# Four of eight row blocks turned by VectorE and through DRAM instead of by TensorE, and the first layer in a new order

## What is computed

```python
h = relu(layernorm(x))
q, k, v = h @ Wq + bq, h @ Wk + bk, h @ Wv + bv
adj = zeros(N, N); adj[src, dst] = 1
a = (q @ k.T) / sqrt(512) * adj + (1 - adj) * -1e6
x = x + softmax(a) @ v
h = relu(layernorm(x))
agg = segment_sum(h[src], dst) / max(degree, 1)
x = x + h + alpha * (agg @ W.T + b)
```

## Time and profile before

| | us |
|---|---|
| median of 3 runs | 228.92 (228.65 to 229.41) |
| the profiled execution | 228.71 |
| its span | 226.9 |
| first projection G0 of the first layer starts | 26.77 |
| first scores start | 85.44 |

### The profile page before, as it was taken

How to read it: one execution, slowest core, us unless ns; L and a number is a source line. 1 busy time by engine, 2 the same in 40 slices (tenths; PEclk the granted TensorE clock), 3 DMA queues, 4 the chain that set the end, 5 groups by cost and what they waited for, 6 DMA issues and landing times.

```text
span 226.9 us, 3216 instructions
## 1 busy us (share of the span) xinstructions
PE 222.7 (98%) x1226; PEld 180.9 (80%) x1226; DVE 172.7 (76%) x282; ACT 81.2 (36%) x143; POOL 80.2 (35%) x106
## 2 busy tenths in 40 slices
PE   8999999999999999999999999999999999999995
PEld 6376788888888888888888888888888888888884
DVE  5898999999998962679799999999565772172223
ACT  3589929554222322221443262423241402250000
POOL 4286134720000019991106583751761506000000
DMA  6999301000000002046545334253305000002222
GB/s 179 328 392 395 145 3 48 0 0 3 0 3 0 0 3 95 0 104 185 158 126 169 78 110 118 90 162 75 114 0 184 1 3 0 3 0 76 110 94 94
DMA packets 12913, 20.70 MB, mean 91 GB/s; under 512 B 1760, under 2 KB 6880, under 8 KB 12768
## 3 DMA queue, kind: packets, MB, share of 16 engines
q1 hardware_dynamic: 12032, 20.06, 27.1%
q10 hardware_dynamic: 864, 0.40, 0.6%
HBM read 14.17 MB, written 6.29 MB: 90 GB/s over the span
## 4 chain that ended last, share of the span: by engine, by line
PE 93%; DVE 3%; DMA 2%; ACTq 0%; issue 0%; DVEq 0%
PE bank L865 20%; PE bank L856 16%; PE bank L855 16%; PE bank L854 16%; PE bank L1022 13%; PE bank L881 8%; PE bank L938 3%; DMA dst_i<-in_dst 2%; PE bank L915 2%; DVE ohL L593 1%; DVE ohW L597 1%; DVE key_b L583 0%; DVE o_sb L836 0%; ACTq L454 0%; PE bank L888 0%; DVE key_t L581 0%
## 5 line engine op out<-in xcount | busy, mean ns | idle before, releaser
L597 DVE TENSOR_TENSOR ohW<-iotaW,key_b 128x1280 bf16<-128x1280 bf16 (+4 forms) x33 | 25.3, 766 | 0.0
L593 DVE TENSOR_TENSOR ohL<-iotaL,lo_b 128x1024 bf16<-128x1024 bf16 x33 | 22.8, 690 | 3.2 <-PE bank L881 3.1
L854 PE MATMUL bank<-hT_hi,GT_hi 128*128 128x512 f32 x64 | 25.0, 391 | 0.0
L856 PE MATMUL bank<-hT_hi,GT_lo 128*128 128x512 f32 x64 | 24.9, 389 | 0.0
L856 PE MATMUL bank<-V_hi,pT_lo 128*128 128x512 f32 x64 | 24.9, 389 | 0.0
L854 PE MATMUL bank<-V_hi,pT_hi 128*128 128x512 f32 x64 | 24.9, 389 | 0.0
L855 PE MATMUL bank<-V_lo,pT_hi 128*128 128x512 f32 x64 | 24.9, 389 | 0.0
L1022 PE MATMUL bank<-A,h_hi 128*128 128x512 f32 x64 | 24.9, 389 | 0.0
L855 PE MATMUL bank<-hT_lo,GT_hi 128*128 128x512 f32 x64 | 24.9, 389 | 0.0
L1022 PE MATMUL bank<-A,h_lo 128*128 128x512 f32 x64 | 24.9, 389 | 0.0
L881 PEld LDWEIGHTS bank<-ohW,ohL 128*128 128x128 bf16 x334 | 18.6, 98 | 4.3 <-issue 3.5
(11 more groups left out here) (132 smaller groups left out, 501.3 us busy)
## 6 DMA issues: line engine op xcount, KB each, us to landing
turned_dram<-turned SPq DMA_DIRECT2D x32, 128.0 KB, 2.3
pT_f<-turned_dram SPq DMA_DIRECT2D x8, 512.0 KB, 3.2
xs<-in_x SPq DMA_DIRECT2D x4, 512.0 KB, 8.1
out_dram<-o_sb SPq DMA_DIRECT2D x7, 256.0 KB, 2.0
wv_raw<-in_wv SPq DMA_DIRECT2D x1, 1024.0 KB, 11.3
wk_rows<-in_wk SPq DMA_DIRECT2D x1, 1024.0 KB, 13.0
wq_rows<-in_wq SPq DMA_DIRECT2D x1, 1024.0 KB, 12.0
wt_raw<-in_wT SPq DMA_DIRECT2D x1, 1024.0 KB, 5.2
```

The lines of the kernel that those rows point to most:

```text
L593: nc.vector.tensor_tensor(ohL[:, q % RING, :, :].rearrange("p b (m two) -> p b m two", two=2), bcast(iotaL[:, :].rearrange("p (m two) -> p ...
L597: nc.vector.tensor_tensor(ohW[:, q % RING, :, 0:row].rearrange("p b (m two) -> p b m two", two=2), bcast(iotaW[:, 0:row].rearrange("p (m t ...
L854: mm(out, lhs[0][a], rhs[0][b], start=(first and k == 0), stop=False)
L856: last = mm(out, lhs[1][a], rhs[0][b], start=False, stop=(final and k == len(pairs) - 1))
```

## The change

Row blocks 0 to 3 are turned as before. For blocks 4 to 7 (TURNED = 4) PE has no T step. DVE gets a step "turn n": it waits for the normalised block and turns it in 32x32 blocks into rows_tn, one of two buffers; from the third on it also waits until the block two before is out. SP, behind the way back of u and ahead of bv_sb, waits for it, sends it out to rows_d in four transfers, waits for these, and fetches it back into hT_f in one. ACT's T step waits for that landing and rounds from hT_f (SBUF) to hT_hi, DVE's T step subtracts from hT_f; both go through a pattern by quarters. rows_tn lies where wq_raw was, hT_f (one buffer per block) where wk_raw was and where GT_hi of the second half will be. PE no longer uses banks 6 and 7 for these four. All four orders are new: among others PE counts 12 batches before G0 where it counted 11, M1 moves ahead of T0, V3 to V6 come before G4, gsum comes before usum.

```diff
-PE_ORDER = ("Mk0 Mk1 c3 bb M0 c2 T0 M1 M2 c2 T1 c2 M3 T2 T3 c2 G0 G1 G2 G3 V0 T4 c2 V1 T5 c3 V2 V3 c3 V4 T6 T7 V5 c3 G4 c1 "
-           "G5 c3 G6 c2 V6 V7 c2 G7 c3")
-ACT_ORDER = ("sum0 sum1 sq0 sq1 k0 sum2 rows0 sq2 k1 M0 sum3 T0 rows1 sum4 M1 sq3 M2 k2 rows2 T1 rows3 k3 M3 T2 T3 sum5 wv0 "
-           "sq4 sum6 k4 G0 sum7 wv1 sq5 G1 rows4 sq6 G2 k5 rows5 G3 V0 rows6 T4 sq7 T5 V1 V2 k6 k7 V3 k8 rows7 V4 T6 T7 k9 "
-           "k10 V5 k11 G4 k12 G5 G6 k13 V6 V7 k14 k15 G7")
-DVE_ORDER = ("o8 T0 M0 bb o2 M1 T1 o1 M2 M3 T2 T3 usum gsum o1 G0 wv0 wv1 G1 o2 dot0 o1 G2 dot1 o1 dot2 dot3 T4 G3 V0 o3 "
-           "dot4 o1 V1 dot5 T5 o1 V2 T6 T7 o1 V3 o3 V4 o1 V5 o2 dot6 o1 dot7 o1 G4 G5 G6 o3 V6 V7 G7")
-POOL_ORDER = ("sum0 sum1 sq0 sum2 sq1 sum3 sq2 sum4 sq3 sum5 sq4 sum6 sum7 sq5 sq6 sq7")
+PE_ORDER = ("Mk0 Mk1 c3 bb M0 c2 M1 c3 T0 T1 M2 c2 T2 M3 T3 c2 G0 G1 G2 G3 c2 V0 V1 c1 V2 c3 V3 V4 V5 c3 V6 c3 G4 c2 G5 "
+            "c2 G6 V7 c2 G7 c3")
+ACT_ORDER = ("sum0 sq0 sum1 sum2 k0 sum3 sq1 sq2 k1 rows0 rows1 sum4 k2 M0 T0 sq3 T1 rows2 M1 M2 rows3 T2 sum5 k3 M3 T3 "
+             "sq4 sum6 sq5 wv0 sum7 sq6 rows4 wv1 G0 sq7 G1 k4 G2 k5 rows5 rows6 T4 k6 G3 rows7 V0 T5 V1 T6 V2 k7 k8 V3 V4 "
+             "T7 k9 k10 V5 k11 k12 V6 G4 G5 G6 V7 k13 G7 k14 k15")
+DVE_ORDER = ("o8 bb o3 T0 T1 o1 M0 M1 M2 M3 T2 T3 gsum o1 usum turn4 o1 wv0 G0 wv1 G1 o1 G2 o1 turn5 o1 turn6 o1 dot0 G3 "
+             "dot1 V0 dot2 o1 V1 turn7 T4 T5 o1 dot3 o1 V2 T6 dot4 o3 V3 T7 o2 V4 dot5 o2 V5 dot6 V6 o1 G4 o3 dot7 o1 G5 "
+             "G6 V7 G7")
+POOL_ORDER = ("sum0 sq0 sum1 sum2 sq1 sum3 sum4 sq2 sq3 sq4 sum5 sum6 sum7 sq5 sq6 sq7")
+TURNED = 4
...
+        hT_f = [place(f"hT_f{i}", [P, P // 32, KD, 32], F32, r_G + (8 + 2 * i) * KB) for i in range(NT - TURNED)]
+        rows_tn = [place(f"rows_tn{i}", [P, P // 32, KD, 32], F32, r_G + (24 + 2 * i) * KB) for i in range(2)]
...
+        def row_quarters(tile, n):
+            return tile[:, :, n * P:(n + 1) * P].rearrange("p k (a q) -> p a k q", a=NQ)
...
+            for i, n in enumerate(range(TURNED, NT)):
+                sp.wait_ge(rows_turned, i + 1)
+                for a in range(NQ):
+                    sp.dma_start(rows_d[i % 2].rearrange("(b q) a f -> a q b f", b=NQ)[a],
+                                 rows_tn[i % 2][a * Q:(a + 1) * Q, :, :, :].rearrange("q b k c -> q b (k c)")).then_inc(rows_out[i % 2], 16)
+                sp.wait_ge(rows_out[i % 2], 16 * NQ * (i // 2 + 1))
+                sp.dma_start(hT_f[i][:, :, :, :].rearrange("p a k c -> p a (k c)"), rows_d[i % 2]).then_inc(hT_in[i % 2], 16)
...
+                elif step == "T" and n >= TURNED:
+                    i = n - TURNED
+                    act.wait_ge(hT_in[i % 2], 16 * (i // 2 + 1))
+                    nc.scalar.activation(row_quarters(hT[0], n), hT_f[i][:, :, :, :], ACT.Copy).then_inc(hT_hi, 1)
...
+                elif step == "turn":
+                    i = n - TURNED
+                    dve.wait_ge(relu, n + 1)
+                    if i >= 2:
+                        dve.wait_ge(rows_out[i % 2], 16 * NQ * (i // 2))
+                    nc.vector.transpose(rows_tn[i % 2][:, :, :, :].rearrange("p b k c -> p k b c"),
+                                        h1[:, n, :].rearrange("p (k b c) -> p k b c", k=KD, b=NQ)).then_inc(rows_turned, 1)
+                elif step == "T" and n >= TURNED:
+                    dve.wait_ge(hT_hi, n + 1)
+                    nc.vector.tensor_tensor(row_quarters(hT[1], n), hT_f[n - TURNED][:, :, :, :], f(row_quarters(hT[0], n)),
+                                            ALU.subtract).then_inc(hT_lo, 1)
```

More of the change, by code:

```diff
@@ L125, with gnn_kernel @@
 NPROJ = len(PROJ)
-def gnn_kernel(nc, x_d, src_d, dst_d, wqT_d, wkT_d, wk_d, wq_d, bqrow_d, bkrow_d, u_d, turned_d, wv_d, wT_d, bq_d, bk_d, bv_d, b_d, alpha_d, out_d):
+def gnn_kernel(nc, x_d, src_d, dst_d, wqT_d, wkT_d, wk_d, wq_d, bqrow_d, bkrow_d, u_d, turned_d, rows_d, wv_d, wT_d, bq_d, bk_d, bv_d, b_d, alpha_d, out_d):
     with ExitStack() as ctx:
@@ L283, in gnn_kernel @@
         blocks_turned, pT_hi, pT_lo = sem("blocks_turned"), sem("pT_hi"), sem("pT_lo")
+        rows_turned = sem("rows_turned")
+        rows_out = [sem(f"rows_out{i}") for i in range(2)]
+        hT_in = [sem(f"hT_in{i}") for i in range(2)]
         turned_out = [sem(f"turned_out{i}") for i in range(2)]
@@ L1110 @@
             args.append([nc.dram_tensor(f"turned_dram{i}", (P, P // 32, N // 4), _mybir.dt.float32).ap() for i in range(2)])
+            args.append([nc.dram_tensor(f"rows_dram{i}", (P, P // 32, D // 4), _mybir.dt.float32).ap() for i in range(2)])
         args.append(nc.dram_tensor(f"in_{name}", a.shape, _mybir.dt.from_np(a.dtype), kind="ExternalInput").ap())
```

## The result

| | us | ratio to before |
|---|---|---|
| kernel before, beside the three series (6, 32 and 12 executions) | 228.75, 228.81, 228.95 (227.91 to 229.53) | |
| changed kernel, first series, 6 executions | 227.70 (227.10 to 228.01) | 0.9944 [0.9926, 0.9961] |
| the same kernel, second series, 11 | 227.80 (227.16 to 228.01) | 0.9957 [0.9941, 0.9974] |
| the same kernel, third series, 6 | 227.31 (226.84 to 227.96) | 0.9933 [0.9911, 0.9956] |

The change makes the kernel 0.45 to 0.65% faster, some 1.2 us by the medians of all 23 executions (227.66) and of the 50 of before (228.86). I had forecast 228.4, a gain of 0.5 us, and "the same" (228.2 to 229.6) as the likeliest outcome.

A forecast was written before the change was run, and what follows sets the result against it. TensorE bounds the kernel, with VectorE beside it in the first layer. Of 1.65 us taken off TensorE, 0.8 to 1.4 return as waits, a gain of 0.2 to 0.9, taken as 0.5: 228.92 - 0.5 = 228.4 us, range 227.5 to 229.8.

The forecast's parts named there:

- TensorE's loss, 1.65 us: First layer: sixteen transposes leave TensorE, 0.43 + 0.43 + 0.79 = 1.65 us, all on the path.
- VectorE's instructions: First layer: four block transposes at 0.62 us, 2.5 in all; low parts of blocks 4 to 7 stay at 0.60.
- the doubled transpose: Rival: a 512-column block transpose costs 1.24 us, VectorE bounds the first layer with 2.5 us more; 230.6 us, chance 0.05.
- The trip through DRAM: Blocks 4 to 7: out 3.65 us, in 3.0, so a block is back 6.65 us after its turning.
- the slower-side rival: Block 5's DRAM trip holds VectorE at V1; each microsecond beyond 6.65 adds one; 229.9 at the longest wait, chance 0.13.
- The waits that come back: First layer: TensorE's new waits return 0.8 to 1.4 us of the 1.65, a gain of 0.2 to 0.9.
- Batch 10 behind k3: Near 26 us TensorE waits 0.1 to 1.0 us for ScalarE's eviction of group 3, behind rows3 and GpSimd's norms.
- V0, 0 to 0.5: At about 40 us TensorE's V0 waits 0 to 0.5 us for G0's low part and wv_lo, behind usum and turn4.
- Batch 23: TensorE wants its one-hots at 64.9 us and gets them at 65.1, a wait of 0.1 to 0.3.
- Batch 30 behind the eviction of bank 1: TensorE waits 0.2 us for bank 1, which ScalarE evicts behind V7, itself waiting for the last dot product.
- The bill of room: VectorE up to its last one-hot: 4.15 us wanted against 3.1 of waits, so about 1 of the 1.65 must return.
- full removal: Rival: lower-bound VectorE instructions, norms at 1.1, no wait over 0.2; gain 0.9 to 1.65, 227.3 to 228.0, chance 0.22.

The follow-up runs named there:

- tensor_turns: The changed kernel with its new orders kept, but TensorE again turning all eight blocks and no trip through DRAM; 229.14 us, ratio 1.0016.
- thin_turns: The changed kernel with each block transpose taking only 128 of its 512 columns, the rest zeros, transfers at full size; 227.33 us, ratio 0.9924.
- third_look: The changed kernel unedited, run and profiled once more, the third series; 227.31 us, ratio 0.9933.
- again: The changed kernel unedited, run and profiled once more, the second series; 227.80 us, ratio 0.9957.
- v0_early: The changed kernel with usum moved behind wv_lo and G0's low part, and block 4 sent out ahead of u; 227.49 us, ratio 0.9938.
- trip5: The changed kernel with block 5 sent out twice, one after the other, making its trip 3.1 us longer; 230.78 us, ratio 1.0069.
- old_order: The changed kernel with blocks 4 to 7 still through DRAM, but the engine orders of before with the turn steps put in; 231.38 us, ratio 1.0129.

## Why the prediction was wrong, step by step

**TensorE's loss, 1.65 us: right.** 1.6 us between tensor_turns and the changed kernel from V0 on, 1.67 between the two profiles of one form, 68.58 against 68.61 us in thin_turns. Against the 6.2 us that the Trainium skill's figure for a TensorE transpose would have given (page "VectorE: DVE Perf Modes", section "The three transpose paths"), an estimate of 16 times 390 ns, the row decided rightly.

**VectorE's instructions: right.** The turns took 0.70 us, 0.62 to the next start, and the low parts through the quartered pattern 0.60:

```profile
L675 DVE STREAM_TRANSPOSE rows_tn<-h x4: 703/704/709, 36.6 to 54.3; 128x512 f32<-128x512 f32 x4
```

```profile
54.30 0.70 DVE L675 STREAM_TRANSPOSE rows_tn<-h 128x512 f32<-128x512 f32 x1
54.92 1.25 DVE L679 TENSOR_TENSOR hT_lo<-hT_f,hT_hi 128x512 fp32r<-128x512 f32 x2
```

Half of the 1240 ns of the earlier trace rows was nearly the right price, and the doubled transpose is out. (Two of my sums were 0.1 off: VectorE's path to turn5 adds up to 45.5 and not 45.6, and the doubled transpose to 230.5 and not 230.6. Neither carries anything.)

**The trip through DRAM: a little too dear.** Forecast 6.65 us, with 3.65 for the way out. SP's timeline (issues of one block's way out and in) and ScalarE's copy give block 5:

```profile
46.14 1.76 SPq L356 DMA_DIRECT2D rows_dram<-rows_tn  x4
49.23 0.34 SPq L359 DMA_DIRECT2D hT_f<-rows_dram  x1
49.62 1.88 SPq L356 DMA_DIRECT2D rows_dram<-rows_tn  x4
54.45 0.34 SPq L359 DMA_DIRECT2D hT_f<-rows_dram  x1
```

```profile
52.14 0.64 ACT L513 ACTIVATE hT_hi<-hT_f 128x512 fp32r<-128x512 f32 x1 [1.49 <-DMA hT_f<-rows_dram]
```

3.1 us out (46.14 to 49.23), 2.9 in, 6.0 in all. The four ways out took 3.85, 3.09, 4.83 and 3.27, so my 3.65 was a fair mean, and block 6 shows that 4.8 happens (it has the slack for it). The tightest spot was named rightly (VectorE at V1's low part, then V4's last term), but it has about 0.6 us of slack, not none; the slower-side rival is real, begins there, and did not occur.

**The waits that come back: this is the step that failed.** Forecast 0.8 to 1.4 us, measured 0.28 to 0.66 in three profiles. The kinds of wait were right; their sum was too large.

- *Batch 10 behind k3, 0.1 to 1.0, and V0, 0 to 0.5.* Both exist, 0.38 (with 0.17 at T2 ahead of it and some 0.1 to 0.2 of slower starts) and 0.44. The prediction said that the one grows as the other shrinks; the profiles say it more strongly: with either in full the other is close to nothing. The norms took 1.1 to 2.4 us from var_e to the end of nmr, and k3 was done at 25.76 in third_look and at 27.26 in the first profile, with the forecast at 26.4 to 27.3. The early waits, by tensor_turns, are no cost of the turning at all.
- *Batch 23, 0.1 to 0.3: absent.* In third_look its one-hots are ready at 63.58 + 0.81 = 64.39, and TensorE, whose group of three starts at 63.48, wants them 1.18 later, at 64.66. I had them 0.2 behind. Counted from VectorE's first one-hot (8.88 before, 8.27 here) they come where I had them, 56.1 us on for 56.2; it is TensorE that wants them later, 56.4 us on for 56.0. The wait at V0 holds TensorE back by 0.44 us and not VectorE, and my sum seems not to have carried that forward; its single steps are not written out, so this reading is argued.
- *Batch 30 behind the eviction of bank 1, 0.2: absent*, by 0.1. ScalarE's eviction behind V7 is over at 82.86 + 0.59 = 83.45, TensorE's batch 30 starts at 83.55.

The two readings, batch 23 in third_look and the eviction in the first profile:

```profile
63.48 1.98 PE L914 MATMUL bank<-ohW,ohL 128*128 128x160 bf16 x29
...
63.58 0.81 DVE L619 TENSOR_TENSOR ohW<-iotaW,key_b 128x1280 bf16<-128x1280 bf16 x1
```

```profile
82.37 0.60 ACT L538 ACTIVATE V_hi<-bank 128x512 fp32r<-128x512 f32 x1 [4.56 <-DVE c_f L693]
82.86 0.59 ACT L521 ACTIVATE A<-bank 128x512 fp32r<-128x512 f32 x1
```

The two at the end are 0.3 to 0.5 us of my sum and cost nothing. That leaves 0.5 to 0.9 for batch 10 and V0 together, where the profiles show 0.28 to 0.66. Together that is the difference.

**The bill of room failed too.** It said 4.15 us are wanted against 3.1 of waits in VectorE's queue up to its last one-hot, so 1 us must come back. It took the distance from the last one-hot to the first scores for granted. This is the last one before, and after:

```profile
82.88 0.55 DVE L597 TENSOR_TENSOR ohW<-iotaW,key_b 128x768 bf16<-128x768 bf16 x1
```

```profile
83.26 0.55 DVE L619 TENSOR_TENSOR ohW<-iotaW,key_b 128x768 bf16<-128x768 bf16 x1
```

Before, it ended at 83.43, 2.01 us ahead of the first scores; after, at 83.81, 0.94 ahead of them, and TensorE, which wants it for its last batch, still doesn't wait. That is 1.07 us of room that my bill didn't have. And the new order puts two low parts of G behind the last one-hot where one of V stood, so that of VectorE's 2.5 us more only 1.8 lie ahead of it (from the first one-hot to the last: 74.55 us less 3.1 idle before, 74.92 less 1.65 idle after, 71.45 and 73.27 of work). The bill that comes out even is: 1.82 us more to do, 0.70 less time, against 1.45 less idleness and 1.07 less margin. All that VectorE has left of idle time up to there, in the first profile, are two waits for ScalarE; the 3.1 for the ring are gone:

```profile
DVE V_lo L715 <- ACT V_hi L538: 1.3, 1, 1.3
...
DVE M_lo L706 <- ACT M_hi L528: 0.3, 1, 0.3
```

**The choice between the cases.** The profile after looks like my forecast in form (the early waits, T5 on ScalarE at 52.14 as said, block transposes at 0.70, VectorE's one idle spot of 0.34 us between 21 and 68) and like "full removal" in its size: that case had 227.3 to 228.0 and a chance of 0.22. What spoke for it and weighed too little is that each wait in my sum makes the next one smaller. I had allowed for that between batch 10 and V0 and, as far as the record shows, not further down.

**What stays open.** The profiles give back 0.3 to 0.7 us of 1.65, that is a gain of 1.0 to 1.35, and the medians 1.0 to 1.6; the two agree within what three series can tell. Of the three profiles of the unedited kernel one had the early form, and no execution without a profile tells its form, so the two forms' times can't be set side by side. Early edges, by which third_look's expectation told the forms apart, don't decide it alone: tensor_turns has the early form (0.16 and 0.38 ahead of G0) with its first one-hot at 8.31. What fits is how late x is against the edges. ScalarE's first sum starts 1.51 us behind the first one-hot in the first profile and 1.45 in tensor_turns, the two with the early form; in again, third_look, v0_early, thin_turns and trip5, which begin with the same orders and haven't got it, by 0.76 to 1.31. No run delayed a load on purpose, so this is a fit and not shown.

## What to carry over

When an order is walked through on paper, a wait of one engine is time that the other has gained: carry it forward before pricing the next wait, and don't add up waits that feed on the same slack. Before concluding from "more work than room", count the margin at the end of the stretch too, and what the new order puts behind it. Taking work off the engine that bounds the kernel is worth its price only in an order in which the engine beside it delivers early enough: here the move in the old order, placed as in old_order, cost 1.3%, the order alone brought nothing, and both together gained 0.5%.

## What the runs showed that I had not expected

**Some executions with a late transfer cost more than the stall.** In trip5 TensorE is busy for 1.03 us of the 3 between 55 and 58. Behind that the granted clock falls (the columns are those of the earlier trace rows, with the clock third from the end):

```profile
52.00:55.00 3.00, 3.00 (x15) 2.48 (x14) 1.60 (x4) 0.07 (x1) 0.00 (x0) 1.00 0.55 139
55.00:58.00 3.00, 1.03 (x5) 0.53 (x3) 1.91 (x4) 1.05 (x2) 0.00 (x0) 1.00 0.39 118
58.00:60.00 2.00, 1.98 (x8) 1.62 (x9) 2.00 (x4) 1.36 (x3) 0.00 (x0) 0.89 0.55 134
60.00:62.00 2.00, 2.00 (x6) 1.57 (x5) 2.00 (x5) 0.24 (x1) 0.00 (x0) 0.50 0.26 40
62.00:64.00 2.00, 2.00 (x18) 1.48 (x17) 1.67 (x4) 0.00 (x0) 0.00 (x0) 0.76 0.26 95
64.00:86.00 22.00, 22.00 (x183) 18.53 (x181) 19.79 (x35) 7.26 (x13) 0.00 (x0) 1.00 0.00 1
```

0.50 is 1.2 GHz where 1.00 is 2.4. At the lower level for (0.11 x 2 + 0.50 x 2 + 0.24 x 2) / 0.50 = 3.4 us, TensorE does half the work, which is 1.7 us lost. That is most of the 2.2 us between the medians of the two kinds of execution (a mean granted clock of 0.993 with 231.2 to 231.8 us, 0.998 to 1.000 with 229.1 to 230.4). So the same late transfer costs 1.8 us in one execution (229.47, the median of those five, less 227.66) and 4.0 in the next (231.68). In old_order's profile a stretch with 1.54 us of idle TensorE in 6 was followed by no drop:

```profile
60.00:66.00 6.00, 4.46 (x41) 3.69 (x40) 5.97 (x11) 1.42 (x3) 0.00 (x0) 1.00 0.15 44
66.00:74.00 8.00, 8.00 (x68) 6.61 (x67) 7.42 (x12) 1.47 (x3) 0.00 (x0) 1.00 0.01 2
```

That the stall brings the fall on is not shown. One of old_order's four executions (233.21) and one of thin_turns' six (231.04, the others 226.95 to 227.69) have the same mean granted clock of 0.993, and thin_turns' profile has no wait of TensorE over 0.3 us from 9 us on. There is no profile of either execution. None of the 23 of the changed kernel is under 0.998.

**The edges' landing moves by 1.4 us between executions.** VectorE's first one-hot lies between 8.27 and 9.67 us in the twelve profiled executions, by the wait for dst_i alone (1.19 to 2.59 us), and C follows it, from 14.87 to 15.98. The times of the kernel before spread by 1.5 us (227.91 to 229.43), about as much. The three profiles of the changed kernel have spans of 226.2, 225.4 and 225.3, which against the one of before, 226.9, would be a gain of 0.7 or of 1.6 us, as it happens; the marks C, G and S take most of that out.
